# A four-layer decoder on one core: the combining weights of an expert pair in one transfer, and plain downward products in every second step of the last mixture of experts

## The reference, cut to what matters

```python
scores = sigmoid(xf @ gate_w.T)                     # routing: top groups, then top experts; cw is 0 for experts not chosen
hg = einsum('nh,eih->nei', xf, Wg)
hu = einsum('nh,eih->nei', xf, Wu)
act = silu(hg) * hu
y = einsum('nei,ne,ehi->nh', act, cw, Wd)           # cw: combining weight of token n and expert e
...
shared = silu(xf @ Ws_g.T) * (xf @ Ws_u.T) @ Ws_d.T
```

## Time and profile before

| | |
|---|---|
| time, 3 runs | 2438.49 us median (2436.98 to 2446.38) |
| profiled execution | 2446.44 us, of which the profile's span is 2444.7 us |
| PE busy | 2141.9 us (88%) |
| DVE busy | 1735.3 us (71%) |
| POOL busy | 1174.9 us (48%) |
| granted PE clock, mean | 0.926 of full speed |
| DMA queue of SP | 64712 packets, 159.50 MB, 27.7% of 16 engines |

### The profile page before, as it was taken

How to read it: one execution, slowest core, us unless ns; L and a number is a source line. 1 busy time by engine, 2 the same in 40 slices (tenths; PEclk the granted TensorE clock), 3 DMA queues, 4 the chain that set the end, 5 groups by cost and what they waited for, 6 DMA issues and landing times. The chain is left out here.

```text
span 2444.7 us, 37814 instructions
## 1 busy us (share of the span) xinstructions
PE 2141.9 (88%) x12822; PEld 1482.2 (61%) x12822; DVE 1735.3 (71%) x3653; ACT 1214.2 (50%) x2508; POOL 1174.9 (48%) x1354
## 2 busy tenths in 40 slices
PE   6998779578999976658999999999999977869888
PEld 3666557455788854455666666666666645548655
DVE  5778678655788865665777777778766764479498
ACT  6888545223566652234444444544444433444455
POOL 5332028001699940117766776667665610004298
PEclk8999889867999988768999999999999998989899
DMA  1000015000766600012442434333433331000184
GB/s 49 2 3 2 7 48 123 7 6 21 172 154 153 155 21 20 1 68 39 89 102 74 105 72 106 76 102 82 93 91 73 83 78 41 0 1 1 41 180 108
DMA packets 64904, 161.92 MB, mean 66 GB/s; under 512 B 7995, under 2 KB 19003, under 8 KB 57416
## 3 DMA queue, kind: packets, MB, share of 16 engines
q1 hardware_dynamic: 64712, 159.50, 27.7%
HBM read 156.46 MB, written 3.01 MB: 65 GB/s over the span
## 5 line engine op out<-in xcount | busy, mean ns | idle before, releaser
L2361 PE MATMUL bank<-l2h_og,l2h_wo 128*128 128x512 f32 x512 | 260.2, 593 | 1.6 <-DVE LNT L2622 1.6
L2471 ACT ACTIVATE l2h_pr<-twin,l2h_nmx 128x512 f32<-128x512 f32 x256 | 176.0, 688 | 152.1 <-PE bank L2350 105.4
L2463 ACT ACTIVATE l2h_prT<-bank 128x512 f32<-128x512 f32 x256 | 151.6, 592 | 195.0 <-PE bank L2350 195.0
L1177 POOL TENSOR_TENSOR l1m_hid_lo<-l1m_hid,l1m_hid_hi 128x512 fp32r<-128x512 f32 x128 | 209.5, 1657 | 46.4 <-ACT l1m_hid_hi L1110 46.1
L2625 DVE TENSOR_REDUCE l2h_nmx<-twin 128x2 f32<-128x1024 f32 x128 | 156.0, 1219 | 93.3 <-PE twin L2339 93.2
L2700 POOL TENSOR_TENSOR l2h_vs<-l2h_vg 128x256 f32<-128x256 f32 x256 | 192.9, 753 | 20.3 <-DVE l2h_vg L2598 20.3
L2598 DVE TENSOR_TENSOR l2h_vg<-bank,l2h_gv 128x512 f32<-128x512 f32 x256 | 174.6, 682 | 34.4 <-POOL l2h_vs L2700 21.8
L2610 DVE TENSOR_TENSOR l2h_og<-bank,l2h_gt 128x512 f32<-128x512 f32 x256 | 172.8, 678 | 3.8 <-PE bank L2361 2.7
L2695 POOL TENSOR_TENSOR l2h_plain<-l2h_plain,l2h_rotated 128x512 f32<-128x512 f32 x64 | 82.5, 1289 | 172.9 <-DVE l2h_rotated L2591 172.9
L2350 PE MATMUL bank<-ident,l2h_pr 128*128 128x128 f32 x1024 | 160.8, 280 | 0.0
L2350 PEld LDWEIGHTS bank<-ident,l2h_pr 128*128 128x128 f32 x1024 | 116.7, 140 | 66.8 <-issue 43.1
(11 more groups left out here) (608 smaller groups left out, 5940.1 us busy)
## 6 DMA issues: line engine op xcount, KB each, us to landing
l2h_gt<-l2m_gate_rows SPq DMA_DIRECT2D x128, 512.0 KB, 7.4
l1m_c<-l1m_weights SPq DMA_DIRECT2D x62, 512.0 KB, 6.5
l3m_c<-l3m_weights SPq DMA_DIRECT2D x30, 512.0 KB, 6.6
l0m_c<-l0m_weights SPq DMA_DIRECT2D x14, 512.0 KB, 6.7
l1m_w<-in_l1m_pairs SPq DMA_DIRECT2D x32, 192.0 KB, 6.5
l2h_fresh<-in_l2m_wqkv SPq DMA_DIRECT2D x8, 768.0 KB, 4.3
l2h_wo<-in_l2m_wo SPq DMA_DIRECT2D x8, 512.0 KB, 3.8
l0m_w<-in_l0m_pairs SPq DMA_DIRECT2D x8, 192.0 KB, 5.7
```

What stands on the lines that cost most here:

```text
L1177: nc.gpsimd.tensor_tensor(hid_lo[:, h % RING, :], hid[:, h % 4, :], hid_hi[:, h % RING, :], ALU.subtract)\
L2361: nc.tensor.matmul(ybank[:, :], wo[s][:, e, :], og[:, e % 4, :], start=(e == 0), stop=(e == E - 1))\
L2463: nc.scalar.activation(prT[:, j // 2 % 2, h, :, j % 2 * P:(j % 2 + 1) * P], tbank[:, :].rearrange("p (c q) -> p c q", c=TPB), ACT.Copy).th ...
L2471: nc.scalar.activation(pr[:, h, :], sbank[:, h, :], ACT.Exp, bias=nmx[:, k % 2, h:h + 1], accum_out=rs[:, g % 2, t, h:h + 1]).then_inc(exp ...
```

## The change

In all three stages the two transfers of a pair become one that fills 128 partitions; its source names the two rows of `weights`, each repeated 64 times, and the counts that DVE waits for are halved to suit. In `l3m` alone, the even steps make the product downward with plain fp32 operands: `w_down[s]`, the third block of the pair's weights, widened from bf16 to fp32 by ACT, times `hid` itself. Even steps so have neither `hid_hi` nor `hid_lo`, and one matmul downward where odd steps have two. `hid` gets 8 buffers in `l3m`. SP also waits for the widening before it fetches the slot's next weights.

```diff
+        HELD = 8 if half_weights else 4
+        hid = st.sb("hid", [P, HELD, S])
+        w_down = [st.sb(f"w_down{i}", [P, P]) for i in range(SLOTS)] if half_weights else None
+        w_whole = [st.sem(f"w_whole{i}") for i in range(SLOTS)] if half_weights else None
...
+        def whole(h):
+
+            return half_weights and h % 2 == 0
+
+        def rounded_until(h):
+
+            return (h + 1) // 2 if half_weights else h + 1
...
                 def first(c):
                     sp.wait_ge(cw_stored[c], 16)
-                    for e in range(2):
-                        sp.dma_start(cslot[0][e * I:(e + 1) * I, c * S:(c + 1) * S],
-                                     weights[e:e + 1, c * S:(c + 1) * S].broadcast_to([I, S])).then_inc(cw_first[c], 16)
+                    rows = weights[0:2, c * S:(c + 1) * S]
+                    sp.dma_start(cslot[0][:, c * S:(c + 1) * S], rows.unsqueeze(1).broadcast_to([2, I, S])).then_inc(cw_first[c], 16)
...
                 def fetch_cw(s, turn):
                     row = turn * 2 * SLOTS + 2 * s
-                    for e in range(2):
-                        sp.dma_start(cslot[s][e * I:(e + 1) * I, :], weights[row + e:row + e + 1, :].broadcast_to([I, N]))\
-                            .then_inc(cw_here[s], 16)
+                    sp.dma_start(cslot[s][:, :], weights[row:row + 2, :].unsqueeze(1).broadcast_to([2, I, N])).then_inc(cw_here[s], 16)
...
                         sp.wait_ge(w_low[s], turn + 1)
+                        if half_weights:
+                            sp.wait_ge(w_whole[s], turn + 1)
                         fetch(s, turn + 1)
...
+                    if whole(h):
+                        if blk == 0:
+                            pe.wait_ge(w_whole[s], turn + 1)
+                        pe.wait_ge(hidden, PRE + h + 1)
+                        out = nc.tensor.matmul(acc[blk][:, :], w_down[s][:, :], hid[:, h % HELD, :], start=False, stop=h >= STEPS - B)
+                    else:
+                        pe.wait_ge(hid_high, rounded_until(h))
+                        out = product(acc[blk][:, :], w, slice(2 * P, 3 * P), hid_hi[:, h % RING, :], hid_lo[:, h % RING, :], False,
+                                      h >= STEPS - B, rounded_until(h))
...
+                def widen_down(s, turn):
+
+                    act.wait_ge(arrived[s], 16 * turn + 16)
+                    nc.scalar.activation(w_down[s][:, :], wslot[s][:, 2 * P:3 * P], ACT.Copy).then_inc(w_whole[s], 1)
+
                 def round_hidden(h):
 
+                    if whole(h):
+                        return
...
-                    if split_at(h) and not half_weights:
+                    if split_at(h):
                         act.wait_ge(down_done, PRE + h - DLAG - 1)
-                        split_weights(*split_at(h))
+                        if half_weights:
+                            widen_down(*split_at(h))
+                        else:
+                            split_weights(*split_at(h))
...
-                    pool.wait_ge(hid_high, h + 1)
...
+                    if not whole(h):
+                        pool.wait_ge(hid_high, rounded_until(h))
...
-                        dve.wait_ge(cw_first[blk], 32)
+                        dve.wait_ge(cw_first[blk], 16)
                     elif blk == 0:
-                        dve.wait_ge(cw_here[s], 32 * turn + 32 * (s > 0))
+                        dve.wait_ge(cw_here[s], 16 * turn + 16 * (s > 0))
...
-                    if h >= 4:
-                        dve.wait_ge(hid_low, h - 3)
+                    if h >= HELD and whole(h):
+                        dve.wait_ge(down_done, PRE + h - HELD + 1)
+                    elif h >= HELD:
+                        dve.wait_ge(hid_low, rounded_until(h - HELD))
```

More of the change, by code:

```diff
@@ L903, in expert_ffn @@
         prod = st.sb("prod", [P, 2 * S])
-        hid = st.sb("hid", [P, 4, S])
+        HELD = 8 if half_weights else 4
+        hid = st.sb("hid", [P, HELD, S])
+        w_down = [st.sb(f"w_down{i}", [P, P]) for i in range(SLOTS)] if half_weights else None
+        w_whole = [st.sem(f"w_whole{i}") for i in range(SLOTS)] if half_weights else None
         hid_hi, hid_lo = st.sb("hid_hi", [P, RING, S], F32R), st.sb("hid_lo", [P, RING, S], F32R)
@@ L1015, in shared_down @@
                     pe.wait_ge(hidden, g + 1)
-                    nc.tensor.matmul(acc[blk][:, :], shared[:, e, 2 * P:3 * P], hid[:, g % 4, :], start=(e == 0), stop=False)\
+                    nc.tensor.matmul(acc[blk][:, :], shared[:, e, 2 * P:3 * P], hid[:, g % HELD, :], start=(e == 0), stop=False)\
                         .then_inc(down_done, 1)
@@ L1033, in down @@
                 def down(h):
-                    _, s, blk = place(h)
+                    turn, s, blk = place(h)
                     w = (w_hi[s], None if half_weights else w_lo[s])
-                    pe.wait_ge(hid_high, h + 1)
-                    out = product(acc[blk][:, :], w, slice(2 * P, 3 * P), hid_hi[:, h % RING, :], hid_lo[:, h % RING, :], False,
-                                  h >= STEPS - B, h + 1)
+                    if whole(h):
[7 more added lines that the diff above has]
+                                      h >= STEPS - B, rounded_until(h))
                     out.then_inc(closed if h >= STEPS - B else down_done, 1)
@@ L1109, in round_hidden @@
                         act.wait_ge(down_done, PRE + h - RING + 1)
-                    nc.scalar.activation(hid_hi[:, h % RING, :], hid[:, h % 4, :], ACT.Copy).then_inc(hid_high, 1)
+                    nc.scalar.activation(hid_hi[:, h % RING, :], hid[:, h % HELD, :], ACT.Copy).then_inc(hid_high, 1)
                 def take(c):
@@ L1135, in _ @@
                         split_weights(g, 0)
+                    if g < SLOTS - 1 and half_weights:
+                        widen_down(g, 0)
                 for c in range(B):
@@ L1173, in _ @@
                 for h in range(STEPS):
-                    pool.wait_ge(hid_high, h + 1)
[L1175 to L1178, removed]
+                    if not whole(h):
+                        pool.wait_ge(hid_high, rounded_until(h))
+                        if h >= RING:
+                            pool.wait_ge(down_done, PRE + h - RING + 1)
+                        nc.gpsimd.tensor_tensor(hid_lo[:, h % RING, :], hid[:, h % HELD, :], hid_hi[:, h % RING, :], ALU.subtract)\
+                            .then_inc(hid_low, 1)
                     if split_at(h):
@@ L1195, in shared_product @@
                     dve.wait_ge(gated, g + 1)
-                    if g >= 4:
-                        dve.wait_ge(down_done, g - 3)
-                    nc.vector.tensor_tensor(hid[:, g % 4, :], ubank[g % AHEAD][:, :], gate[:, g % 2, :], ALU.mult).then_inc(hidden, 1)
+                    if g >= HELD:
+                        dve.wait_ge(down_done, g - HELD + 1)
+                    nc.vector.tensor_tensor(hid[:, g % HELD, :], ubank[g % AHEAD][:, :], gate[:, g % 2, :], ALU.mult).then_inc(hidden, 1)
                 dve.wait_ge(loaded, 16 * len(loads))
@@ L1220, in _ @@
                     dve.wait_ge(multiplied, h + 1)
-                    if h >= 4:
-                        dve.wait_ge(hid_low, h - 3)
+                    if h >= HELD and whole(h):
+                        dve.wait_ge(down_done, PRE + h - HELD + 1)
+                    elif h >= HELD:
+                        dve.wait_ge(hid_low, rounded_until(h - HELD))
                     elif h == 0:
                         dve.wait_ge(down_done, PRE)
-                    nc.vector.tensor_tensor(hid[:, h % 4, :], p, cslot[s][:, blk * S:(blk + 1) * S], ALU.mult).then_inc(hidden, 1)
+                    nc.vector.tensor_tensor(hid[:, h % HELD, :], p, cslot[s][:, blk * S:(blk + 1) * S], ALU.mult).then_inc(hidden, 1)
                 for c in range(B):
```

## The result

The changed kernel takes 3163.51 us (median of 4 runs, 3159.37 to 3172.93), the kernel before 2439.95 us on the same occasions. The ratio is 1.2966, with a 95% interval of 1.2927 to 1.3006: slower by 30%. The profiled execution took 3172.93 us, with a span of 3171.1 us. The forecast was 3205 us with its own range of 3120 to 3340.

What follows compares the result with a forecast made beforehand. POOL was taken to bound the last stage before, and two-engine transfers all three stages after. Delays of 757 us plus 9 us of tails on the profiled 2446.4 us gave 3212, as median 3205 us; own range 3120 to 3340, overall 2410 to 3340.

Steps and rivals of the forecast that it cites:

- POOL's beat in the last stage: In l3m, POOL's four hid_lo and the w_hi cast fill 7.25 us a pair and set the stage's pace.
- the room of the transfers: A pair's combining weights hold sixteen engines 4.8 us of 7.25 us, a spare factor of 1.5 to 1.7.
- The step that decided: The joined source begins with 2, so its transfer in all three stages runs on two engines, not sixteen.
- The rate: Each of the two engines carries about 25 GB/s, so a pair's combining weights take 21.0 us.
- the sum: 757 us of delays and 9 us of tails on the profiled 2446.4 us; 3205 us as median.
- the forecast delays: Later landing of the last pair's weights: 106 us in l0m, 427 in l1m, 224 in l3m, together 757.
- the tails: The last five steps or so of each stage run slower at a lowered PE clock: 9 us for three.
- Hidden plain products: The even steps' plain products in l3m, worth 7.7 us alone, count 0 behind transfers of 21.0 us.
- The signs in the profile: In the stages: DMA share near 0.12, about 50 GB/s, prod waiting some 700 us for c, lower PE clock, 21 us beat.
- C: Rival for the joined transfers: two engines at 13.3 GB/s each, 39.4 us a pair, 4250 us; chance 0.10.
- B: Rival for the joined transfers: sixteen engines still at 217 GB/s, no difference, 2430 to 2445 us; chance 0.04.
- A: Rival for the joined transfers: sixteen engines at 393 to 414 GB/s, 21 us gained with plain products, 2418 us; chance 0.16.

Runs made afterwards that it cites:

- e1: Plain downward products alone, with two transfers a pair as in the kernel before: 2428.23 us, ratio 0.9945 to the kernel before.
- e3: e2 with the 64 copies outermost in the source and the partitions renumbered, no plain products: 2434.39 us, ratio 0.9963 to the kernel before.
- e7: e2 with each row stored twice in DRAM, so that the source begins with 4: 2630.16 us, ratio 1.0768 to the kernel before.
- e8: e2 with each row stored four times in DRAM, so that the source begins with 8: 2487.26 us, ratio 1.0179 to the kernel before.
- e2: The kernel before with the joined transfer alone, without the plain products: 3164.66 us, ratio 1.2957 to the kernel before.
- e5: e2 with the first expert's row alone filling all 128 partitions, the second's left out: 2436.15 us, ratio 0.9975 to the kernel before.
- e4: The changed kernel with the source begun by the 64 copies, as in e3: 2421.43 us, ratio 0.9918 to the kernel before.
- e9: e2 bringing only half of the tokens from the second turn on, half of the bytes: 2732.91 us, ratio 1.1193 to the kernel before.
- e10: e2 bringing 32 copies of each row, not 64, from the second turn on: 2735.47 us, ratio 1.1195 to the kernel before.

## Why the prediction was right

**The bound.** POOL's beat in the last stage and the room of the transfers were read rightly. e1 confirms the beat: with half of POOL's subtractions gone, PE took over.

**The step that decided,** the number of engines, could not be read from the trace, only argued. The Trainium skill, "DMA: Bandwidth & Descriptors", section "Why a DMA increments its semaphore by 16 and not by 1", stood behind it with its rule of the largest number up to 16 that divides both slowest dimensions. The share of 0.13 in the changed kernel and the turn by e3 show it. e7 and e8, at shares of 0.26 and 0.51, show that it is a rule in the outermost size of the source: 2, 4, 8 and 64 gave 2, 4, 8 and 16 engines. e7 and e8 keep the layout of e2, so the other numbering of the partitions in e3 is not what did it. Sizes other than powers of two were not tried, nor a destination that begins with fewer than 64 partitions.

**The rate.** The sum took 25 GB/s an engine; in a window with nothing else it was 26.5. Over whole stages, expert weights included, the two engines carried 25.6, 25.8 and 26.1 GB/s each. That is why 40 us are missing from the sum, and not the 66 us that 26.5 throughout would have taken off (524,288 bytes in 19.8 us in place of 21.0, 56 times). Counted as in the sum, from a stage's first issue to the last pair's first `prod` (521.9, 1386.6 and 3153.2 us; before 420.4, 874.9 and 2428.1), the forecast delays of 106, 427 and 224 us came out as 102, 406 and 209: 717 us in place of 757. What is left of the 726 us is 9 us, as the forecast had for the tails, though part of it stands between the stages. So the difference between 3205 and 3163.5 us is in the size of one term, the rate; the mechanism is not touched.

**Hidden plain products.** Right: e2 and the changed kernel are 1 us apart.

**The signs in the profile.** The share (0.14 to 0.16 with the expert weights, for 0.12) and the rate (57 to 60 GB/s, for about 50) came near the forecast. The clock fell (0.67 to 0.74 in the stages), and the beat was 20 to 21 us. Wrong was where the wait would stand. I forecast some 700 us of `prod` waiting for `c`; it was 182 us, and 581 us for `gate`. I had counted the expert weights as bytes on the two engines, but not followed who stands behind them: ACT, in order, with the next `gate` after it. It cost nothing, since the same two engines release both: e2's last stage has no such wait and takes as long.

**Rivals.** C (13.3 GB/s) is refuted by the rate of the run itself, and its reason by e5. B's condition, sixteen engines held at 217 GB/s, did not come about: e3 reached 438. A is what e4 does: forecast 2418, measured 2421.4. That it came so near is luck in part, since its parts were off both ways: the transfers gave 9 us, not 13, the plain products 13, not 7.7. Here PE's step was priced too high. I had charged 0.34 us for the first matmul of each step, where PE had stood idle just before; in e1, where it does not, the first matmul after a rounded product is 0.24 us, two steps take 3.18, and the steady beat falls by 0.85 us (7.25 to 6.40), not 0.5. The last stage is 117.4 - 105.9 = 11.5 us shorter. The claim that A decides from about six engines on was wrong: it took for granted that every engine always gives 25 GB/s, and eight engines, at 14 to 16 each for the first pairs, still lost 1.8%.

## What to carry to other kernels

Fewer, larger transfers are not better by themselves: look at what each access pattern begins with, and keep a large dimension there (64 and 128 filled all sixteen engines here); where two rows are to be spread over partitions, put the copies outside and renumber the partitions. A DMA share that stood still at two sixteenths for whole stages was the mark of this, whatever engine the waits named. And two transfers that each fill half of the partitions gain rate by joining, 438 for 217 GB/s here; it is worth much only where DMA is the bound, and here it gave 9 us.

## What the runs showed of the hardware that I had not expected

SP's issue of a DMA took 18 to 20 us when two engines had the transfers of several pairs queued, 0.6 us otherwise. So the engine that issues can be held, not only the data. At equal bytes it was held longer when an engine had 64 rows of 4 KB a pair (e9) than when it had 32 rows of 8 KB (e10), 9.6 against 3.9 us in the median of the last stage; here is one issue of each in `l1m`:

```profile
807.46 9.55 SPq L965 DMA_DIRECT2D l1m_w<-in_l1m_pairs  x1
```

```profile
813.17 1.10 SPq L965 DMA_DIRECT2D l1m_w<-in_l1m_pairs  x1
```

That points to room counted in rows and not in bytes; how many there is room for was not measured.

Engines are not equal in rate at every split. With 2 engines each gave 26.5 GB/s, with 16 over 128 partitions 26.1, with 16 over 64 partitions 13.3. With 4 it was 17, and with 8 it was 14 to 16, while a stage's first pairs came in. Later they gave more: 24 in e7 (115 GB/s at a share of 0.30), and up to 23 at the end of e8's last stage. Why 4 and 8 are slower at first stays open. That engines writing partitions 32 apart share a way in would have halved e10's rate, and did not; other pairings of partitions were not tried. Also open is why halves of the tokens reach 335 GB/s and not 438 on sixteen engines, when on two engines (e9) the same rows of 4 KB lost nothing.
